# A recurrent block with an FP4 feed-forward gate: the second feed-forward product as three fp32r products, and a new order of the stages

## The reference

```python
xn = layernorm(x)
# branch s
x0 = causal_dwconv(rmsnorm(xn)) @ pw.T + b + xn           # 3 taps, then 256x256
hidden, gate = split(rmsnorm(x0) @ gru_w.T)               # 256 -> 2x256
h_t = sigmoid(-gate_t)*h_(t-1) + sigmoid(gate_t)*g(hidden_t)   # along the 512 tokens
x2 = h + x0
a = gelu(rmsnorm(x2) @ ff_w1.T + b1)                      # ff1: 256 -> 1024
s = a @ ff_w2.T + b2 + x2                                 # ff2: 1024 -> 256
# branch g: both operands of each product rounded to FP4 in blocks of 16
u = silu(fp4(xn) @ fp4(w_gate).T) * (fp4(xn) @ fp4(w_up).T)    # gate/up: 256 -> 704
g = silu(fp4(u) @ fp4(w_down).T)                          # down: 704 -> 256
out = x + s * g
```

## Time and profile before

| | |
|---|---|
| time, median of 3 runs | 1176.81 us (1176.54 to 1176.89) |
| the profiled execution: its time | 1177.03 us |
| its span, first to last instruction | 1175.2 us |
| mean granted TensorE clock | 0.979 of full speed |
| TensorE matmuls (PE) | 1098.3 us busy, 93% of the span |
| VectorE (DVE) | 864.0 us busy, 74% |
| ScalarE (ACT) | 550.1 us busy, 47% |
| GpSimd (POOL) | 143.3 us busy, 12% |
| chain of work that ended last | PE 76%, DVE 16%, ACT 4% |

### The profile page before, as it was taken

The page is one execution under the profiler, slowest core; times in us unless marked ns, Lnnn a source line. Parts: engine busy times, 40 slices in busy tenths (PEclk is TensorE's granted clock), DMA queues, the critical chain, the costliest instruction groups (busy, mean ns, idle before and its releaser), DMA issues.

```text
span 1175.2 us, 16619 instructions
## 1 busy us (share of the span) xinstructions
PE 1098.3 (93%) x6306; PEld 967.7 (82%) x6306; DVE 864.0 (74%) x1638; ACT 550.1 (47%) x887; POOL 143.3 (12%) x122
## 2 busy tenths in 40 slices
PE   3467999999999999999999999999999999999998
PEld 2355988889898888989888898988889898888987
DVE  6777686868868686886868788686877868687755
ACT  3235354554535455453545445354554545545441
POOL 3010020101102010110201011020101102010010
PEclk9587999999999999999999999999999999999999
DMA  6000001010100101010010101001010100100000
GB/s 228 1 0 19 19 14 42 1 54 1 37 18 10 46 1 54 1 37 18 6 50 1 55 1 37 19 1 55 1 51 5 36 18 2 54 1 32 5 18 19
DMA packets 29358, 31.35 MB, mean 27 GB/s; under 512 B 1120, under 2 KB 28512, under 8 KB 29280
## 3 DMA queue, kind: packets, MB, share of 16 engines
q1 hardware_dynamic: 20000, 21.04, 5.8%
q10 hardware_dynamic: 9280, 9.26, 2.6%
HBM read 21.90 MB, written 8.39 MB: 26 GB/s over the span
## 4 chain that ended last, share of the span: by engine, by line
PE 76%; DVE 16%; ACT 4%; issue 2%; DMA 0%; POOL 0%; ACTq 0%; DVEq 0%; POOLq 0%
PE gu_ps L854 39%; PE w_ps L854 27%; PE w_ps L917 3%; DVE hqt_lo L470 3%; DVE x L505 2%; DVE hq L392 2%; DVE q_amax L366 2%; PE gu_ps L900 2%; PE w_ps L861 1%; ACT hqt_hi L731 1%; PE w_ps L872 1%; PE gu_ps L861 1%; DVE q_y L378 1%; PE w_ps L900 1%; DVE cand L503 1%
## 5 line engine op out<-in xcount | busy, mean ns | idle before, releaser
L854 PE MATMUL w_ps<-w,act 128*128 128x256 f32 x960 | 217.1, 379 | 0.0
L854 PEld LDWEIGHTS w_ps<-w,act 128*128 128x128 f32 x960 | 177.7, 190 | 21.7
L454 DVE TENSOR_TENSOR hid<-sl,gu_ps 128x352 f32<-128x352 f32 x128 | 65.7, 514 | 172.7 <-ACT sl L720 170.6
L854 PE MATMUL gu_ps<-gu_hi,xq_hi 128*128 128x352 f32 x512 | 168.8, 330 | 1.0 <-DVE gu_lo L513 1.0
L854 PE MATMUL gu_ps<-gu_lo,xq_hi 128*128 128x352 f32 x512 | 166.0, 324 | 0.0
L854 PE MATMUL gu_ps<-gu_hi,xq_lo 128*128 128x352 f32 x512 | 165.9, 324 | 0.0
L854 PE MATMUL w_ps<-dn_hi,hqt_hi 128*128 128x256 f32 x384 | 119.6, 311 | 8.5 <-DVE hqt_lo L470 8.5
L720 ACT ACTIVATE sl<-gu_ps 128x352 f32<-128x352 f32 x128 | 59.3, 463 | 123.7 <-PE gu_ps L854 122.1
L758 ACT ACTIVATE act<-gu_ps,cols 128x512 f32<-128x512 f32 x128 | 86.4, 688 | 54.5 <-PE gu_ps L854 54.3
L326 POOL TENSOR_TENSOR inv_rms<-ss_row,neg_half 128x4 f32<-128x4 f32 x32 | 40.7, 1271 | 581.9 <-DVE ss_row L480 581.9
L854 PE MATMUL gu_ps<-xs_hi,w_hi 128*128 128x512 f32 x256 | 106.2, 415 | 3.1 <-DVE xs_lo L494 3.1
(11 more groups left out here) (115 smaller groups left out, 2197.9 us busy)
## 6 DMA issues: line engine op xcount, KB each, us to landing
x_in<-x_dram SPq DMA_DIRECT2D x16, 512.0 KB, 4.6
x_res<-x_dram ACTq DMA_DIRECT2D x16, 512.0 KB, 3.9
out_dram<-o SPq DMA_DIRECT2D x15, 512.0 KB, 3.2
act<-w_t_dram SPq DMA_DIRECT2D x1, 1024.0 KB, 13.1
w<-w_t_dram SPq DMA_DIRECT2D x1, 1024.0 KB, 15.6
act<-w_down_dram SPq DMA_DIRECT2D x1, 704.0 KB, 11.1
hid<-w_gate_dram SPq DMA_DIRECT2D x1, 640.0 KB, 6.4
hid<-w_up_dram SPq DMA_DIRECT2D x1, 640.0 KB, 9.3
```

Source lines behind the costliest of these rows:

```text
L454: V.tensor_tensor(hid[:, t, h * HALF:(h + 1) * HALF], sl[:, h, :], gu_ps[:, h, 1, 0:HALF], ALU.mult).then_inc(hid_ready, 1)
L854: done = M.matmul(psum, l, r, start=first and i == 0, stop=last and i == len(terms) - 1)
```

## The change

- `ff2` takes both operands as high part and remainder in fp32r, so each of its 8 products becomes three matmuls. ScalarE makes `act_hi` (`gelus_high`, 8 copies of 128x512 a chunk) and VectorE `act_lo` (`gelus_low`, 8 subtractions of 128x512 a chunk). Calls of `gelus_high` alternate with the first four gelus and stand behind `front_xq` for the other four. `gelus_low` stands ahead of `hidden` of tile 0 (five tiles) and of tile 2 (three) of the next body; in the last body all eight stand behind the outputs. `w2` is split once, in the prologue.
- Buffers share homes: `act_lo` lies where `act1` is, `act_hi` where the loaded `w2_f` was, `take` and `sqs` in `xs`, `y` in `cand`, `x2` is written to `x1`, `q_m` to `q_e`, and `x_res` has one buffer, which the SP queue loads behind each store.
- gate/up goes part by part: `gate_up(c, t, 0)` makes the whole gate of a tile (704 columns in two banks) and `gate_up(c, t, 1)` the whole up part. `silu_gate` and `hidden` become one instruction of 704 columns each. The gate part of a tile waits for the `silu` of the tile before, the up part for its `hidden`.
- On TensorE `down(c-1, 2)` stands behind the whole `gate_up` of tile 3; behind gru come ff2 of tiles 0 and 1, `sum_squares`, `down(c-1, 3)`, `spread_scale`, then ff2 of tiles 3 and 2. On VectorE the subtractions and roundings around `hidden` of tiles 2 and 3 and around the recurrence are put in another order, and `hidden_low` of tile 3 stands behind both halves of the recurrence. On ScalarE `silu_f(c-1, 3)` stands behind `front_xc`.

```diff
+        def shared_home(first, second):
+            with nc.sbuf_tensor(*first) as one:
+                pass
+            return one, sb(*second)
...
-        w2 = sb("w2", [P, KF, D])
+        w2_hi = sb("w2_hi", [P, KF, D], F32R)
+        w2_lo = sb("w2_lo", [P, KF, D], F32R)
...
-        x_res = sb("x_res", [P, 2, T, D])
+        x_res = sb("x_res", [P, T, D])
...
+        sqs = xs[:, 0, :]
...
-        take = sb("take", [P, KD, L])
+        take = xs
         cand = sb("cand", [P, KD, L])
-        x2 = sb("x2", [P, KD, L])
+        y = cand
...
+        act1, act_lo = shared_home(("act1", [P, KF, L], F32), ("act_lo", [P, KF, L], F32R))
+        w2_f, act_hi = shared_home(("w2_f", [P, KF * D], F32), ("act_hi", [P, KF, L], F32R))
...
+        q_m = q_e
...
-        scaled_weights = ((ld_gru, gru_f, gru_hi, gru_lo), (ld_w1, w1_f, w1_hi, w1_lo))
+        halves = lambda w: w[:].rearrange("p (a k) n -> p a (k n)", a=KD)
+        split_weights = ((ld_gru, gru_f, gru_hi, gru_lo), (ld_w1, w1_f, w1_hi, w1_lo),
+                         (ld_w2, w2_f, halves(w2_hi), halves(w2_lo)))
...
+                sp.dma_start(x_res[:], x_v[c + 1]).then_inc(xres_ready, 16)
+            sp.dma_start(x_res[:], x_v[0]).then_inc(xres_ready, 16)
...
-            def hidden(c, t, h):
-                dve.wait_ge(silu_ready, 2 * T * c + 2 * t + h + 1)
-                V.tensor_tensor(hid[:, t, h * HALF:(h + 1) * HALF], sl[:, h, :],
-                                gu_ps[:, h, 1, 0:HALF], ALU.mult).then_inc(hid_ready, 1)
+            def hidden(c, t):
+                dve.wait_ge(silu_ready, T * c + t + 1)
+                dve.wait_ge(gu_done, 2 * (T * c + t) + 2)
+                V.tensor_tensor(hid[:, t, :].rearrange("p (h n) -> p h n", h=2), sl[:],
+                                gu_ps[:, 1, :, 0:HALF], ALU.mult).then_inc(hid_ready, 1)
...
+            def gelus_low(c, tiles):
+                for j in tiles:
+                    dve.wait_ge(acthi_ready, KF * c + j + 1)
+                    V.tensor_tensor(act_lo[:, j, :], act1[:, j, :], act_hi[:, j, :].bitcast(F32),
+                                    ALU.subtract).then_inc(actlo_ready, 1)
...
-                s = steps.mark(V.tensor_tensor_scan(x2[:, k, :], keep[:, k, :], cand[:, k, :], 0.0,
+                s = steps.mark(V.tensor_tensor_scan(take[:, k, :], keep[:, k, :], cand[:, k, :], 0.0,
                                                     ALU.mult, ALU.add))
                 dve.wait_ge(dve_step, s)
-                V.tensor_tensor(x2[:, k, :], x2[:, k, :], x1[:, k, :], ALU.add).then_inc(x2_ready, 1)
+                V.tensor_tensor(x1[:, k, :], take[:, k, :], x1[:, k, :], ALU.add).then_inc(x2_ready, 1)
...
-                hidden(c, 0, 0)
-                hidden(c, 0, 1)
+                if tail:
+                    gelus_low(c - 1, range(5))
+                hidden(c, 0)
                 if tail:
                     scales = hidden_scales(c - 1, 2)
-                hidden(c, 1, 0)
                 add_squares(c * 2)
                 if tail:
                     hidden_low(c - 1, 1)
-                hidden(c, 1, 1)
+                hidden(c, 1)
                 if tail:
                     ratios = fp4_ratios(hid[:, 2, :], NBI, scales)
                 else:
                     down_weight(0)
                 clamp_sums(c * 2, w_ps[:, 0, :])
                 if tail:
-                    rounded = fp4_round(NBI, ratios)
-                hidden(c, 2, 0)
-                if tail:
-                    hidden_values(c - 1, 2, rounded)
-                    scales = hidden_scales(c - 1, 3)
-                hidden(c, 2, 1)
-                if tail:
-                    ratios = fp4_ratios(hid[:, 3, :], NBI, scales)
-                    hidden_low(c - 1, 2)
-                else:
+                    hidden_values(c - 1, 2, fp4_round(NBI, ratios))
+                    gelus_low(c - 1, range(5, KF))
+                hidden(c, 2)
+                if not tail:
                     down_weight_low(0)
                     down_weight(1)
                 scaled(c * 2, x1, w_ps[:, 1, :], (x1_ready, KD * (c + 1)))
                 if tail:
+                    scales = hidden_scales(c - 1, 3)
+                    hidden_low(c - 1, 2)
+                scaled_low(c * 2)
+                if tail:
+                    ratios = fp4_ratios(hid[:, 3, :], NBI, scales)
                     dve.wait_ge(dve_step, ratios)
-                hidden(c, 3, 0)
-                scaled_low(c * 2)
-                if tail:
-                    rounded = fp4_round(NBI, ratios)
-                hidden(c, 3, 1)
-                if tail:
-                    hidden_values(c - 1, 3, rounded)
+                hidden(c, 3)
+                if tail:
+                    hidden_values(c - 1, 3, fp4_round(NBI, ratios))
                 else:
                     down_weight_low(1)
                 if front:
                     front_moments(c + 1)
                 recurrence(c, 0)
+                recurrence(c, 1)
                 if tail:
                     hidden_low(c - 1, 3)
-                recurrence(c, 1)
                 add_squares(c * 2 + 1)
                 if tail:
                     output(c - 1, 0, w_ps[:, 0, :])
...
+                    output(c - 1, 3, w_ps[:, 3, :])
                     output(c - 1, 2, w_ps[:, 2, :])
-                    output(c - 1, 3, w_ps[:, 3, :])
...
+                if not front:
+                    gelus_low(c, range(KF))
...
+                    act.wait_ge(x2_ready, KD * c)
...
-            def silu_gate(c, t, halves=(0, 1)):
-                for h in halves:
-                    n = 2 * T * c + 2 * t + h
-                    act.wait_ge(gu_done, n + 1)
-                    if not (isinstance(c, int) and n < 2):
-                        act.wait_ge(hid_ready, n - 1)
-                    A.activation(sl[:, h, :], gu_ps[:, h, 0, 0:HALF], ACT.Silu).then_inc(silu_ready, 1)
+            def silu_gate(c, t):
+                act.wait_ge(gu_done, 2 * (T * c + t) + 1)
+                act.wait_ge(hid_ready, T * c + t)
+                A.activation(sl[:], gu_ps[:, 0, :, 0:HALF], ACT.Silu).then_inc(silu_ready, 1)
...
+            def gelus_high(c, tiles):
+                act.wait_ge(wlo_ready, 3 * KD)
+                for j in tiles:
+                    act.wait_ge(gelu_ready, KF * c + j + 1)
+                    A.copy(act_hi[:, j, :], act1[:, j, :]).then_inc(acthi_ready, 1)
...
+                act.wait_ge(xslo_ready, KD * (2 * c + 1))
+                act.wait_ge(pw_done, KD * (c + 1))
...
-            def keep_x(c, parity):
-                if not (isinstance(c, int) and c < 2):
-                    act.wait_ge(out_ready, c - 1)
-                act.wait_ge(xres_ready, 16 * c)
-                act.dma_start(x_res[:, parity], x_v[c]).then_inc(xres_ready, 16)
...
+                if j == 2:
+                    break
...
-                squares(c * 2 + 1, x2_ready, c, x2)
-                if tail:
-                    silu_f(c - 1, 3)
+                squares(c * 2 + 1, x2_ready, c, x1)
                 if front:
                     front_xc(c + 1)
+                if tail:
+                    silu_f(c - 1, 3)
...
-                gelus(c, range(KF // 2))
+                for j in range(KF // 2):
+                    gelus(c, (j,))
+                    gelus_high(c, (j,))
                 if front:
                     front_y(c + 1)
                 gelus(c, range(KF // 2, KF))
                 hq_columns(c, 0)
                 if front:
                     front_xq(c + 1)
+                gelus_high(c, range(KF // 2, KF))
                 silu_f(c, 0, w_ps[:, 2 if front else 0, :])
-                if front:
-                    keep_x(c + 1, 1 - parity)
...
-            def gate_up(c, t, h):
-                n = 2 * T * c + 2 * t + h
+            def gate_up(c, t, u):
                 if t == 0:
                     pe.wait_ge(xqhi_ready, KD * (c + 1))
                     pe.wait_ge(xqlo_ready, KD * (c + 1))
                     pe.wait_ge(gelu_ready, KF * c)
+                elif u == 0:
+                    pe.wait_ge(silu_ready, T * c + t)
                 else:
-                    pe.wait_ge(hid_ready, n - 1)
+                    pe.wait_ge(hid_ready, T * c + t)
                 tok = slice(t * P, (t + 1) * P)
-                for u in range(2):
+                for h in range(2):
                     cut = slice(u * NI + h * HALF, u * NI + (h + 1) * HALF)
                     for k in range(KD):
-                        last = product(gu_ps[:, h, u, 0:HALF], (xq_hi[:, k, tok], xq_lo[:, k, tok]),
+                        last = product(gu_ps[:, u, h, 0:HALF], (xq_hi[:, k, tok], xq_lo[:, k, tok]),
                                        (gu_hi[:, k, cut], gu_lo[:, k, cut]), k == 0, k == KD - 1)
                 last.then_inc(gu_done, 1)
...
-                pe.wait_ge(hid_ready, 2 * T * (c + 1) - 1 + k)
```

(60 more changed lines are left out.)

19 lines of the change are left out of this document (7 added, 12 removed).

## The result

The kernel after the change takes **1122.1 us** (median of 4 runs, 1120.7 to 1123.8) against 1176.85 for the kernel before beside it: a ratio of 0.953, with a 95% interval of 0.952 to 0.955. Forecast were 1134.2 us and a range of 1125 to 1149.

A forecast was written before the change was run, and what follows sets the result against it. TensorE, busy 67.36 of 68.70 us a chunk, was taken as the bound. Span 1175.2 + 4.9 (prologue) - 1.0 (chunk 0) - 49.5 (15 x 3.3) + 3.0 (epilogue) = 1132.6, so 1134.2 us; range 1125 to 1149.

The forecast's parts named there:

- ff2 is worth its time on TensorE: Steady chunks: TensorE sets the pace; an ff2 tile falls from 3.68 to 3.13 us, 2.2 us a chunk.
- rival (2): ff2 on TensorE: fp32r matmuls run at the pace of serial weight loads, 4.8 us a tile, 1237 us; chance 0.02.
- The stall of 0.57 us: TensorE's wait for `hqt_lo` ahead of `down(c-1, 2)`, each chunk: falls to about 0.1 us (0 to 0.3).
- the stall of 0.77: TensorE's wait for `sqs` ahead of `sum_squares`, each chunk: falls to about 0.1 us (0 to 0.6).
- 1126 (3.8 a chunk, no hold): Lower end of the likeliest case's range: steady chunks gain 3.8 us and the prologue's hold does not come.
- the hold: Prologue: GpSimd's `w2` subtraction until 33.5 us holds VectorE's `q_wide` or tensor_scalars; chain 4.4 to 5.6 us back.
- Rival (1): Steady chunks: VectorE takes the bound over, waits of 1.5 us leave a gain of 1.8 a chunk, 1157 us; chance 0.12.
- Rival (3): Loop gru, recurrence, norm, ff1: the gain is given back, period stays 68.7 us, 1184 us; chance 0.03.
- Prologue: Before the first gate/up: ScalarE's wait for `w2`, extra copies and GpSimd's subtraction add 4.9 us.
- Rival (4): Prologue: the hold does not come, all else as forecast, 1130 us; chance 0.82 together with the likeliest case.
- Chunk 0: First chunk, without ff2: gains about 1.0 us, since `scaled_low` no longer lies behind a `hidden` and gru begins earlier.
- End: Epilogue: ff2(15, 0) begins 3.8 us later behind copies and subtractions, the last ff2 gives 0.6 back: +3.0 us.

The follow-up runs named there:

- order_only: Kernel after the change with ff2 put back to one fp32 product, without its splits; new order, homes and gate/up part by part stay: 1149.4 us, 0.976.
- two_terms: Kernel after the change without ff2's third product (remainder of the gelus with high part of w2), copies and subtractions kept: 1110.9 us, 0.944.
- old_gru_order: Kernel after the change with only the order behind gru put back on the three engines; gate/up stays part by part: 1164.0 us, 0.988.
- split_only: Kernel after the change with gate/up by halves and the three engines' old order; split ff2 and new homes stay: 1179.4 us, 1.002.

## Why the prediction was right and where it failed

- **What bounds the kernel, and that ff2 is worth its time on TensorE: right.** `order_only` against the kernel after puts the split at 66.90 - 64.53 = 2.37 us a chunk; forecast 2.2, bounds 1.9 to 2.4. The four ff2 alone give 4 x 3.68 - 2 x 3.04 - 2 x 3.07 = 2.5, a little above that bound; 0.15 of it goes in the hidden wait ahead of `sum_squares`. The matmuls are 0.118 us apart, the bound with the entry counted once. The weight loads take 0.19 us each and stay hidden: rival (2) falls. By the Trainium skill, page "FP8 and Floating Point Precision", section "TensorE Precision Notes", three passes in place of four would be 2.60 us; measured are 2.82 to 2.85, nearer the 2.91 by `down`'s row.
- **The stalls: this step failed.** "The stall of 0.57 us goes to about 0.1" and "the stall of 0.77 goes to about 0.1" took 1.14 us a chunk; the order is worth 1.80. The forecast left 0.1 us of each stall, and no idle time is printed at either place, which is 0.2. The larger part, 0.46, is the drain and refill at the edges of the two stalls, which the sum had at nothing: I priced a stall at the idle time that the view prints, and `order_only` shows that it costs 0.2 us more. Over 14 periods and the last chunk this term makes 0.66 x 15 = 9.9 us, against 10.7 by which the span beat the forecast. The ff2 term makes 0.17 x 15 = 2.6 more, the rounding of 3.34 to 3.3 another 0.6, and prologue, chunk 0 and end together take 0.8 - 1.3 - 1.8 = -2.3 back.
- **The range failed with it.** Its lower bound of 3.8 a chunk was ff2's 2.4 and the idle time of 1.34; the measured 4.17 lies outside, because drain and refill were in no bound. Both bounds of the range were also added up wrongly. "1126 (3.8 a chunk, no hold)" is by the prediction's own terms 1134.2 - 15 x 0.5 - 4.4 = 1122.3 us, and its bound of 2.0 a chunk is 1134.2 + 15 x 1.3 = 1153.7, above the 1149 that was said to take it in. With the first of these put right the range would have ended right beside 1122.1, but by luck: the hold came, and the chunk gave more than 3.8.
- **Rival (1), VectorE takes the bound over:** it came only as the hidden wait of some 0.15 us a chunk, with no margin left. `two_terms` shows the bound right behind, `old_gru_order` what its crossing costs: 1.7 us a chunk, and 1.5 more by the clock. I had its price as the waits alone.
- **Rival (3), the gain given back in one loop:** not here, but it is what `split_only` did. Of the 2.37 us of gain there, 0.63 went in a longer stall and 1.50 in the clock.
- **Prologue, +4.1 for +4.9.** `xq_lo` starts at 25.71 in place of 23.68, 2.0 us later and not 2.8: instead of waiting for w2, ScalarE found it landed and began the high parts at 20.28. The hold came, in `q_scale` (2.38 us) and in `q_y` (2.52 in place of 0.69); the first was forecast. Less the hold that `q_wide` had before, they make the other 2.1, as forecast. Rival (4) falls.
- **Chunk 0, +0.3 for -1.0.** TensorE's waits in it fell by 1.1 us, as forecast, but its busy time rose from 46.43 to 47.90 us. From the first gate/up on, the clock stayed at 0.50 for 6.0 us in place of some 2.9; why, no run here tells.
- **End, +4.8 for +3.0.** The idle time ahead of ff2(15, 0) is 3.98 us (forecast some 4). The clock fell to 0.50 within it and stayed there behind it, and ff2's 24 matmuls, which lie on the chain, took 4.82 us in place of 2.85. These 2.0 us are the missing 1.8. The chain there, and a window:

```profile
1090.53 0.66 PE gu_ps L993 x2
1091.19 4.82 PE gu_ps L881 x24
```

```profile
1092.00:1094.00 2.00, 2.00 (x12) 2.00 (x11) 2.00 (x3) 0.00 (x0) 0.00 (x0) 0.50 0.00 0
```
